# SyncE reads an expert's row once in the late slots and queues its constants ahead of its weights

## The reference

```
x = LN(x + attention_layer(x))        # 16 heads, relu scores, causal; feed-forward 256 -> 1024 -> 256
e = argmax(x @ centroids.T)           # 8 experts, one for each token
h = relu(LN_e(x) @ w1[e].T + b1[e])   # 256 -> 1024; ln_g, ln_b, b1 are the expert's own
y = x + h @ w2[e].T + b2[e]           # 1024 -> 256
out = LN(x + alpha * y + (1 - alpha) * x)   # alpha = sigmoid(affinity to the chosen centroid)
```

## Time and profile before

| | us |
|---|---|
| median of 3 runs | 895.95 |
| profiled execution | 895.32 |
| its span, first to last instruction | 893.5 |
| PE busy | 847.5 |
| DVE, ACT, POOL busy | 456.8, 354.4, 281.3 |

### The profile page before, as it was taken

How to read it: one execution, slowest core, us unless ns; L and a number is a source line. 1 busy time by engine, 2 the same in 40 slices (tenths; PEclk the granted TensorE clock), 3 DMA queues, 4 the chain that set the end, 5 groups by cost and what they waited for, 6 DMA issues and landing times.

```text
span 893.5 us, 19587 instructions
## 1 busy us (share of the span) xinstructions
PE 847.5 (95%) x7394; PEld 561.3 (63%) x7394; DVE 456.8 (51%) x1334; ACT 354.4 (40%) x591; POOL 281.3 (31%) x392
## 2 busy tenths in 40 slices
PE   8999999999999999999999999999998889889884
PEld 5555575575576476477467468699885557457553
DVE  5474365455365366256277356246874445445442
ACT  1444315415424424423533433232333555455550
POOL 3403111521421422332242062245444334334212
PEclk9999999999999999999999999999999999899997
DMA  6502000100110020020030124235646676677650
GB/s 237 178 3 70 2 1 26 42 31 15 35 49 2 25 72 1 25 72 1 26 119 1 49 74 153 72 121 172 196 147 229 230 275 237 227 280 234 243 190 15
DMA packets 38595, 93.30 MB, mean 104 GB/s; under 512 B 13987, under 2 KB 26916, under 8 KB 30566
## 3 DMA queue, kind: packets, MB, share of 16 engines
q1 hardware_dynamic: 33206, 80.42, 26.0%
q0 software_dynamic: 4864, 11.10, 3.9%
q10 hardware_dynamic: 432, 0.54, 0.3%
HBM read 81.07 MB, written 11.23 MB: 103 GB/s over the span
## 4 chain that ended last, share of the span: by engine, by line
PE 82%; DVE 6%; issue 4%; ACT 2%; DMA 2%; SPq 1%; POOL 1%; another core or an unknown queue 0%; DVEq 0%; ACTq 0%; POOLq 0%
PE ps L597 13%; PE ps L603 12%; PE ps L544 8%; PE ps L568 7%; PE ps L690 7%; PE ps L708 6%; PE ps L730 5%; PE ps L516 3%; PE ps L576 3%; PE ps L443 3%; PE ps L464 3%; PE ps L472 3%; PE ps L754 2%; PE ps L406 2%; ACT arena L1600 2%
## 5 line engine op out<-in xcount | busy, mean ns | idle before, releaser
L603 PE MATMUL ps<-ff2T,hT 128*128 128x256 f32 x512 | 121.0, 384 | 0.2 <-ACT hT L1522 0.2
L597 PE MATMUL ps<-x3x,ff1T 128*128 128x512 f32 x256 | 118.8, 604 | 0.1
L1530 ACT ACTIVATE arena<-ps 128x1536 f32<-128x1536 f32 (+3 forms) x49 | 65.1, 1329 | 128.3 <-DVE arena L997 122.2
L603 PEld LDWEIGHTS ps<-ff2T,hT 128*128 128x128 f32 x512 | 94.3, 190 | 16.3 <-issue 3.4
L997 DVE SCALAR_TENSOR_TENSOR arena<-ps,arena 128x512 f32<-128x512 f32 (+4 forms) x59 | 44.9, 768 | 107.2 <-PE ps L544 64.3
L708 PE MATMUL ps<-w_sb,arena 128*128 x400 | 95.7, 382 | 0.0
L708 PEld LDWEIGHTS ps<-w_sb,arena 128*128 128x128 f32 x400 | 72.2, 190 | 16.0 <-issue 8.2
L1600 ACT ACTIVATE arena<-ps,arena 128x128 f32<-128x128 f32 (+2 forms) x104 | 36.1, 420 | 107.5 <-PE ps L676 70.9
L597 PEld LDWEIGHTS ps<-x3x,ff1T 128*128 128x128 f32 x256 | 45.6, 190 | 52.2 <-issue 49.9
L544 PE MATMUL ps<-arena 32*128 32x512 f32 (+7 forms) x896 | 73.0, 434 | 1.7 <-ACT hT L1016 1.2
L1822 POOL DMA_INDIRECT arena<-token_store,ids x34 | 33.5, 984 | 98.3 <-DMA ids<-slot_table 90.7
(11 more groups left out here) (225 smaller groups left out, 1578.2 us busy)
## 6 DMA issues: line engine op xcount, KB each, us to landing
arena<-in_w SPq DMA_DIRECT2D x27, 1024.0 KB
hT<-in_w SPq DMA_DIRECT2D x16, 1024.0 KB
wts<-in_w SPq DMA_DIRECT2D x9, 1024.0 KB
w_sb<-in_w SPq DMA_DIRECT2D x8, 1024.0 KB, 5.3
token_store<-x SPq DMA_DIRECT2D x8, 520.0 KB
arena<-in_x SPq DMA_DIRECT2D x8, 512.0 KB, 3.8
arena<-in_epack SPq DMA_DIRECT2D x25, 134.0 KB
slot_table<-padid POOLq DMA_DIRECT2D x4, 576.0 KB
```

Source lines behind the costliest of these rows:

```text
L597: last = eng.matmul(ps[:, 6 + m % 2, :], ff1T[:, kd, m * P:(m + 1) * P], xT3[:, kd, :], start=kd == 0, stop=kd == KD - 1)
L603: last = eng.matmul(quarter(6, t), hT[:, m, t * P:(t + 1) * P], ff2T[:, m, :], start=m == 0, stop=m == FM - 1)
L1530: eng.activation(o, i, ACT.Relu).then_inc(s_sa, 1)
```

## The change

SP's part of the late slots is rewritten. Everything else is as it was; PE, ACT, DVE and POOL run the same instructions.

1. The row of the expert is read from `tab` once a slot (three times in a mixed slot, once a part) by the new `slot_sp_rows`, and used for constants and weights. Before, each of the two read it again.
2. For the slots from 4 on the constants come ahead of the weights. Their wait for slot j - 4 so comes ahead of the weights too.
3. `before[j]` is a list, and each place in the ring is waited for just ahead of its own load. Before, the first load waited for the latest of all.

```diff
-            before[j] = max((used[u][-1] for u in w1_of[j] if u in used), default=-1)
+            before[j] = [used[u][-1] if u in used else -1 for u in w1_of[j]]
...
+        def slot_sp_rows(eng, j):
+            if j in MIXED:
+                return [part_entry(eng, j, p, 2, (NE - 1) * P) for p in range(NP)]
+            return [slot_entry(eng, j, 2, (NE - 1) * P)]
+
-        def slot_sp_ep(eng, j):
+        def slot_sp_ep(eng, j, at):
...
-        def slot_sp_w1(eng, j):
+        def slot_sp_w1(eng, j, at):
...
-            else:
-                if before[j] >= 0:
-                    eng.wait_ge(p_l1d, before[j] + 1)
-                if WN in w1_of[j] or WN + 1 in w1_of[j]:
+            for p, u in enumerate(w1_of[j]):
+                if before[j][p] >= 0:
+                    eng.wait_ge(p_l1d, before[j][p] + 1)
+                elif u >= WN:
                     eng.wait_ge(s_f2, 2 * NB)
-            for p, u in enumerate(w1_of[j]):
-                row = part_entry(eng, j, p, 2, (NE - 1) * P) if j in MIXED else slot_entry(eng, j, 2, (NE - 1) * P)
-                eng.dma_start(w1_ring[u], w1[bass.ds(row, P), :]).then_inc(s_w1[u], 16)
+                eng.dma_start(w1_ring[u], w1[bass.ds(at[p], P), :]).then_inc(s_w1[u], 16)
...
-                slot_sp_w1(eng, j)
-                slot_sp_ep(eng, j)
+                at = slot_sp_rows(eng, j)
+                slot_sp_ep(eng, j, at)
+                slot_sp_w1(eng, j, at)
                 if XN <= j + 3 < N_TILE:
                     slot_sp_ids(eng, j + 3)
```

More of the change, by code:

```diff
@@ L1962, in slot_sp_ep @@
             if j not in MIXED:
-                row = slot_entry(eng, j, 2, (NE - 1) * P)
-                eng.dma_start(ep[j % EN][:, 0:EW], epack[bass.ds(row, P), :]).then_inc(d_ep[j % EN], 16)
+                eng.dma_start(ep[j % EN][:, 0:EW], epack[bass.ds(at[0], P), :]).then_inc(d_ep[j % EN], 16)
                 return
             for p, rows in enumerate(PART_ROWS):
-                row, c = part_entry(eng, j, p, 2, (NE - 1) * P), columns_of(p)
-                eng.dma_start(ep[j % EN][:, c:c + 12], epack[bass.ds(row, P), 0:12],
+                c = columns_of(p)
+                eng.dma_start(ep[j % EN][:, c:c + 12], epack[bass.ds(at[p], P), 0:12],
                               allow_slow_non_contiguous=True).then_inc(d_ep[j % EN], 16)
                 eng.dma_start(ep[j % EN][rows, E_B2:E_B2 + H],
-                              epack[bass.ds(row, rows.stop - rows.start), E_B2:E_B2 + H]).then_inc(d_ep[j % EN], 16)
-        def slot_sp_w1(eng, j):
+                              epack[bass.ds(at[p], rows.stop - rows.start), E_B2:E_B2 + H]).then_inc(d_ep[j % EN], 16)
+        def slot_sp_w1(eng, j, at):
             if j == 0:
@@ L2029, in sp_program @@
                         slot_sp_ids(eng, j)
-                    slot_sp_w1(eng, 0)
+                    slot_sp_w1(eng, 0, slot_sp_rows(eng, 0))
                     eng.wait_ge(s_pb, NB)
@@ L2035, in sp_program @@
                     for j in range(EN):
-                        slot_sp_ep(eng, j)
+                        slot_sp_ep(eng, j, slot_sp_rows(eng, j))
             sp_store_x(eng, NB - 3)
@@ L2039, in sp_program @@
             for j in range(1, WN):
-                slot_sp_w1(eng, j)
+                slot_sp_w1(eng, j, slot_sp_rows(eng, j))
             sp_store_x(eng, NB - 2)
```

## The result

The changed kernel takes 882.27 us (median of 4, 882.04 to 883.65), beside 896.47 for the kernel before in the same runs. The ratio is 0.9841, 95% interval 0.982 to 0.9862: 1.6% faster. Its profiled span is 879.9 us against 893.5, so 13.6 us are to be explained; 19.3 had been forecast. The time lies in the recorded range of 863 to 889 us, 6.3 us above the 876 that was named.

What follows compares the result with a forecast made beforehand. A loop through SP, POOL and DVE was to bound short intervals at 18.4 us. Intervals and faster products gain 18.7 us, slot 14 0.6: 19.3 off 895.3 gives 876 us, own range 870 to 882, recorded 863 to 889.

Steps and rivals of the forecast that it cites:

- The new loop: SP's wait for slot j - 4's result, three weights, numbers, POOL, DVE's L1303: 17.9 us, above PE's 16.2; chance 0.58.
- the rival with full DMA engines: Small transfers between the weights stretch the three to 12.5 to 13 us; intervals of 20 us, 885 us; chance 0.19.
- a short interval: Between mixed layers 1 with one full slot between, about 20 us before: forecast 18.4; six of them gain 14.13 us.
- the numbers don't overtake the weights: In SP's queue, numbers cannot count as landed before the weights ahead of them; without this the loop falls to PE's bound.
- the long intervals: The two 25 us intervals with two full slots between lose only slow products: 1.31 us behind slot 18, 1.70 behind 25.
- L730 at 3.64: PE's layer 1 of mixed slots takes 3.64 us after pauses of some 2.2 us, being slow only after 4 us.
- Slot 14: PE starts the first late mixed slot at 684.7 instead of 685.35: 0.6 us gained; 2 us slower at worst.
- The full slots: Slots 5 to 13, weights issued up to 6 us later behind constants: cost nothing, up to 4 us with cover gone.
- That PE bounds: Rival: numbers or weights land faster, so short intervals are PE's own 16.2 us, time 863 us; chance 0.12.
- That nothing comes of it: Rival: the wait for slot j - 4 replaces that for j - 2; some 1 us in six places, 893 us; chance 0.05.
- it gets slower: Rival: mixed slots' numbers need 14.4 us, loop 21.0, full slots lose 0.5 us each: about 901 us; chance 0.06.
- the places one by one: A mixed slot's first two weights may go long before; the queued wait holds them, and only the third waits for j - 2.

Runs made afterwards that it cites:

- The experiment with two weights ahead: Changed kernel, but in slots 21 and 28 two of three weights go ahead of the constants, the third behind them: 878.62 us, ratio 0.9808.
- numbers ahead: Changed kernel with the numbers of slot j + 3 issued between constants and weights in all slots: 888.99 us, ratio 0.9888.
- the four with the loop opened or the wait moved: Places one by one alone on the kernel before 867.70 us; changed kernel with weights before constants 864.21, numbers before weights in some mixed slots 870.92, third weight behind constants 859.51.
- the last kernel: Changed kernel, but in mixed slots two weights go first, then the constants, then the third weight: 859.51 us, ratio 0.9597.
- weights first: Changed kernel with the weights ahead of the constants again, places one by one and rows read once: 864.21 us, ratio 0.9648.

## Why the prediction was right or wrong

**The sign and the mechanism held.** The new loop was the forecast, and the chain shows it term by term. The time alone would not have: 882.3 us lies just beyond the forecast's own range (870 to 882) and nearer to the 885 of the rival with full DMA engines than to 876. The intervals tell them apart, 18.6 us against that rival's 20. From slot 12's L1303 (ends 688.74) to slot 14's (ends 707.92) are 19.2 us, and to slot 16's another 18.6:

| term | forecast | measured |
|---|---|---|
| result of j - 4 to the first weight | 3.5 | 3.5 (688.74 to 692.28, 707.92 to 711.46) |
| first weight to the third's landing | 10.9, 0.5 for traffic | 11.2 (711.46 to 722.67) |
| first weight to numbers landed | 11.3, 0.5 for traffic | 12.3 (692.28 to 704.55); at slots 21, 23 and 28 11.3, 11.6 and 11.1 |
| gather to the end of L1303 | 3.1 | 3.1 (704.81 to 707.92) |
| a short interval | 18.4 | 18.6 in the mean |

Two numbers beside it were off: the DMA share was to go to 0.88 and was 0.75 from 700 to 750 us, and the granted clock was to be 1.00 and was 0.97.

That the numbers don't overtake the weights is borne out, and the two kernels that put them ahead show that the loop hangs on it. In the Trainium skill's "DMA: Bandwidth & Descriptors", section "Queues, rings and completion order", the reason given is that each DMA engine takes its descriptors in ring order and that a semaphore's write lands only after every earlier write of that engine. By that rule, the trace agrees: the numbers landed 12.3 us after the first weight's issue, and PE, waiting for the last of the three weights, started 0.03 us later (704.55, 704.58).

Of the 19.3 us forecast 5.7 did not come: 1.1 in the short intervals (13.0 for 14.1), 0.6 at slot 14, and 4.0 in the long intervals.

**What failed is the step on the long intervals**, in the words "there the loop has a full slot more of time". It was to bring 3.0 us and brought -1.0. I had closed the loop over pairs of mixed slots and not looked at the release across three. Slot 21 waits for slot 17's result. DVE reaches L1303 of slot 17 only behind slot 18's hidden rows, so 5.4 us after slot 18's layer 1 (728.21 to 733.61). Then come 3.9 us to the first weight (737.55) and 11.3 to slot 21's start (748.88): 20.7 us behind that layer 1, where PE alone needs 20.2. A slow L730 in slot 18 (5.34) added 1.7. Slot 28 shows the loop alone. Slot 25's layer 1 took 3.64 and ended at 789.10, slot 24's result came at 795.67, the first weight went at 800.06 and slot 28 started at 811.12: 22.0 us, 1.8 more than PE needs. Of the 4.0 us missed, then, 2.3 are the wait for slots 17's and 24's results with three weights behind it, and 1.7 the clock. The experiment with two weights ahead brought both pauses down to 0.34 us, as where PE bounds.

**L730 at 3.64** was put too low. I had taken pauses of 2 us as harmless. Slots 18 and 23, after 2.25 and 2.45 us, took 5.34, and slot 30, after 2.90, took 4.93. That is 1.7 + 1.7 + 1.3 = 4.7 us over the three (slot 14 took 5.34 as well). In the short intervals that begin with slots 14, 23 and 30 it cost nothing, because the loop that sets their length does not go through PE's layer, and they met the forecast in the mean. In slot 18 it stretched a long interval.

**Slot 14** was to gain 0.6 us and gained nothing: the first weight was issued at 673.72, as worked out (673.6), and PE started 11.6 us after it, not 11.1.

**The full slots** were rightly costed at nothing. Layer 1 of slot 13 starts at 673.83 against 674.00. The cover was thinner than it looked for one order only: numbers ahead, where slot 11's weight stood behind a table.

**The rivals.** That PE bounds was wrong for this kernel, and right for the four with the loop opened or the wait moved, at the 16.2 us worked out for it. That the DMA engines bound the interval as a whole is excluded: the same bytes passed at 301 GB/s in the last kernel. But while three weights pass, the longest term of the loop, they have little room left; at slot 18's weights in the changed kernel the share is 0.97:

```profile
712.00:722.70 10.70, 8.63 (x103) 6.31 (x101) 5.18 (x18) 7.83 (x17) 1.04 (x1) 1.00 0.97 358
```

That nothing comes of it, and that it gets slower, were both wrong; for the latter the numbers would have had to land 14 us after the first weight, and they took 12.3.

**What it left out.** The prediction asked what each edit costs beside the others and named the places one by one as free "long before". It did not draw the conclusion that this part alone, without the wait in front, would reach PE's bound. The changed kernel lies 17 us (weights first) and 22 us (third weight last) above the better orders by the ratios. Most of that is the price of the wait that the constants put ahead of the weights; slot 14's earlier start is 1.6 and 4.5 us of the difference in the profiles, a part of it present before any mixed slot (672.1 and 672.2 against 673.8 at slot 13).

## What to carry to other kernels

A queue in program order passes a wait on to everything behind it. Before a small transfer with a late condition goes ahead of a large one with an early condition, follow what is queued behind both until it comes round to the condition again; if it does, the period is the sum of that loop and not the busiest engine. Put first what may go first, and the small, late-conditioned transfers ahead of only the last large one. And take such a change apart: here one of three edits alone was worth twice the whole.

## What the runs showed of the hardware

TensorE's clock after a pause did not go by the pause's length alone. In the changed kernel pauses of 2.25 and 2.45 us were followed by L730 of 5.34 us, with the granted clock at the lower of its two levels (1.2 GHz) in part:

```profile
723.00:728.30 5.30, 5.30 (x33) 1.59 (x29) 2.85 (x9) 2.25 (x2) 3.96 (x7) 0.68 0.49 154
```

In the kernel with constants first and one wait, a pause of 3.75 us ahead of slot 23 and one of 2.65 ahead of slot 18 were followed by 3.64 us at full clock. The window right behind the first, with the same columns (the 1.00 is the granted clock):

```profile
767.60:771.30 3.70, 3.64 (x33) 1.20 (x33) 1.46 (x4) 1.63 (x2) 2.80 (x6) 1.00 0.26 83
```

What decides between them these runs don't show. A part of the gains is the clock's: the nine L730 sum to 44.9 us before, 39.1 in the changed kernel, and 32.8 where PE hardly waited. With the rows read once and nothing else they sum to 45.1, and one pause of only 2.17 us (slot 30) was followed by 5.34.
